# Ln and Exp over two chunks at once in a graph layer with routed experts: the adjacency stage on ScalarE, with its mask lead and one copy on VectorE moved

## What is computed

```
msg     = layernorm(x) @ W + B                       # x 8192x128
sens    = exp(-(1/adj - 1)**2 / (2 * 0.5**2))        # adj 8192x8192, most entries 0
weights = where(adj < 1, sens, 0)
x       = x + weights @ msg
z       = layernorm(x)
x       = x + layernorm(z + moe(z)) * gamma + beta   # 16 experts, top 2, 128 -> 256 -> 128, relu
```

## Time and profile before

| | us |
|---|---|
| median of 3 runs (1758.34 to 1759.6) | 1759.18 |
| the profiled execution's own time | 1758.88 |
| its span | 1757.1 |
| PE busy, of the span | 1624.8 (92%) |
| ACT busy | 1581.2 (90%) |
| DVE busy | 1525.8 (87%) |
| POOL busy | 430.1 (24%) |
| share of the 16 DMA engines taken by the loads' queue | 61.9% |
| a load of one chunk (1024 KB), from issue to landing, median | 5.3 |

### The profile page before, as it was taken

How to read it: one execution, slowest core, us unless ns; L and a number is a source line. 1 busy time by engine, 2 the same in 40 slices (tenths; PEclk the granted TensorE clock), 3 DMA queues, 4 the chain that set the end, 5 groups by cost and what they waited for, 6 DMA issues and landing times.

```text
span 1757.1 us, 23405 instructions
## 1 busy us (share of the span) xinstructions
PE 1624.8 (92%) x8178; PEld 1080.6 (61%) x8178; DVE 1525.8 (87%) x2278; ACT 1581.2 (90%) x1577; POOL 430.1 (24%) x309
## 2 busy tenths in 40 slices
PE   4889999999999999999999999999999999999840
PEld 3556666566656566656556656566656557999840
DVE  7999999999999999999999999999999994557876
ACT  5889999999999999999989999999999995666752
POOL 0000030303131313131304030303031301117775
PEclk9999999999999999999999999999999999999985
DMA  9447876667666666666867666667666842457653
GB/s 319 146 136 252 251 213 205 187 203 217 200 203 199 195 204 204 202 200 201 230 192 207 203 207 204 189 202 216 203 188 203 230 123 77 149 156 227 193 152 97
DMA packets 208500, 341.91 MB, mean 195 GB/s; under 512 B 18224, under 2 KB 65840, under 8 KB 208256
## 3 DMA queue, kind: packets, MB, share of 16 engines
q1 hardware_dynamic: 200064, 323.30, 61.9%
q0 software_dynamic: 8320, 17.12, 3.2%
HBM read 304.38 MB, written 35.98 MB: 194 GB/s over the span
## 4 chain that ended last, share of the span: by engine, by line
PE 44%; ACT 28%; DVE 12%; issue 11%; POOL 4%; DMA 1%; POOLq 0%; SPq 0%; DVEq 0%; ACTq 0%
PE acc L1033 22%; PE tp L1052 11%; ACT chunk L467 10%; ACT chunk L462 9%; ACT wT L473 8%; PE tp L1082 4%; PE tp L1095 4%; POOL chunk L446 4%; DVE chunk L595 4%; DVE chunk L589 4%; PE tp L1071 1%; PE misc L985 1%; DVE stats L601 1%; DVE msg L650 1%; DMA xs<-in_x_dram 1%
## 5 line engine op out<-in xcount | busy, mean ns | idle before, releaser
L1033 PE MATMUL acc<-wT,msg 128*128 128x512 f32 x2048 | 973.0, 598 | 16.2 <-DVE yT L681 16.2
L595 DVE SCALAR_TENSOR_TENSOR chunk<-chunk 128x2048 f32<-128x2048 f32 x256 | 585.6, 2287 | 98.2 <-ACT chunk L467 98.0
L1052 PEld LDWEIGHTS tp<-ident,chunk 128*128 128x128 f32 x4096 | 484.1, 142 | 226.2 <-issue 214.7
L473 ACT ACTIVATE wT<-tp 128x1024 f32<-128x1024 f32 x512 | 570.4, 1114 | 22.4 <-PE tp L1052 22.4
L589 DVE SCALAR_TENSOR_TENSOR chunk<-chunk 128x2048 f32<-128x2048 f32 x256 | 584.0, 2282 | 1.9 <-DMA chunk<-in_adj_dram 1.9
L1052 PE MATMUL tp<-ident,chunk 128*128 128x128 f32 x4096 | 538.5, 275 | 0.0
L462 ACT ACTIVATE chunk<-chunk 128x2048 f32<-128x2048 f32 x256 | 514.9, 2011 | 11.9 <-DVE chunk L589 11.9
L1033 PEld LDWEIGHTS acc<-wT,msg 128*128 128x128 f32 x2048 | 351.6, 192 | 267.7 <-issue 267.0
L467 ACT ACTIVATE chunk<-chunk 128x2048 f32<-128x2048 f32 x256 | 513.7, 2007 | 0.0
L418 POOL TENSOR_TENSOR pool_carrier<-pool_carrier 1x1 f32<-1x1 f32 x32 | 8.6, 270 | 1232.0 <-DVE row_now L766 1189.5
L428 POOL DMA_INDIRECT rows_in<-y,row_now x128 | 286.6, 2239 | 44.7 <-issue 44.7
(11 more groups left out here) (106 smaller groups left out, 574.8 us busy)
## 6 DMA issues: line engine op xcount, KB each, us to landing
chunk<-in_adj_dram SPq DMA_DIRECT2D x256, 1024.0 KB, 5.3
chunk<-rows_in SPq DMA_DIRECT2D x88, 128.0 KB, 2.1
rows_out<-chunk SPq DMA_DIRECT2D x88, 128.0 KB
y_kept<-y SPq DMA_DIRECT2D x16, 256.0 KB, 6.1
rows_in<-zeros SPq DMA_DIRECT2D x32, 128.0 KB
chunk<-y_kept SPq DMA_DIRECT2D x16, 256.0 KB, 3.4
out_dram<-chunk SPq DMA_DIRECT2D x16, 256.0 KB, 2.6
blobs<-in_L_ffn_w_dram SPq DMA_DIRECT2D x1, 2048.0 KB, 12.0
```

Of the source, the lines that this page charges most:

```text
L473: act.activation(wT[:, (g * PPG + m) % WSLOTS, :], tp[(g * PPG + m) % TSLOTS][:, :], ACT.Exp, scale=-2.0).then_inc(weighted, 1)
L595: dve.scalar_tensor_tensor(out=slot(c), in0=slot(c), scalar=2.0, in1=slot(c), op0=ALU.subtract, op1=ALU.mult).then_inc(squared, 1)
L1033: ins = pe.matmul(acc[:, :], msg[:, n, :], wT[:, (g * PPG + m) % WSLOTS, k * ROWS:(k + 1) * ROWS], start=(n == 0), stop=(n == 2 * PPG - 1))
L1052: ins = pe.transpose(tp[s % TSLOTS][:, t * ROWS + b * P:t * ROWS + (b + 1) * P], chunk[:, c % RING, b, j:j + P], ident[:, :])
```

## The change

From chunk 1 of group 1 on, Ln and Exp run over two neighbouring chunks in one instruction of 4096 elements a partition. Ln of a pair stands in the even step of an odd chunk (chunks c + 3 and c + 4), Exp of a pair in the even step of an even chunk (chunks c + 2 and c + 3); the odd steps have neither. Masks lead by five chunks from group 1 on, with one extra mask at its start. DVE's copy of the finished sum stands before the square of step 1, where it stood before the mask of step 2.

```
-    SQUARE_LEAD, LOG_LEAD, MASK_LEAD = 2, 3, 4
+    SQUARE_LEAD, LOG_LEAD, MASK_LEAD, PAIR_LEAD = 2, 3, 4, 5

+            def two(c):
+                return chunk[:, c % RING:c % RING + 2, :, :].rearrange("p r b j -> p (r b j)")
+
+            def log_two(g, c):
+                act.wait_ge(masked, g * CHUNKS + c + 2)
+                act.activation(two(c), two(c), ACT.Ln, bias=TINY).then_inc(logged, 2)
+
+            def invert_two(g, c):
+                act.wait_ge(logged, g * CHUNKS + c + 2)
+                act.activation(two(c), two(c), ACT.Exp, scale=-1.0).then_inc(inverted, 2)

@@ ScalarE, step m of group g, behind weigh(g, m)
-                    n = c + LOG_LEAD
-                    if not (g == GROUPS - 1 and n >= CHUNKS):
+                    if g == 0 or (g == 1 and c == 0):
+                        n = c + LOG_LEAD
                         (log if k == 0 else invert)(g + n // CHUNKS, n % CHUNKS)
+                    elif k == 0:
+                        n = c + (LOG_LEAD if c % 2 else LOG_LEAD - 1)
+                        if not (g == GROUPS - 1 and n >= CHUNKS):
+                            (log_two if c % 2 else invert_two)(g + n // CHUNKS, n % CHUNKS)

@@ VectorE, step m of group g
-                    if g and m == BEHIND:
+                    if g and m == BEHIND - 1:
                         gate_sum(g - 1)
                     c, k = divmod(m, PAIRS)
-                    n = c + (MASK_LEAD if k == 0 else SQUARE_LEAD)
+                    if g == 1 and m == 0:
+                        mask(g, MASK_LEAD)
+                    n = c + (SQUARE_LEAD if k else MASK_LEAD if g == 0 else PAIR_LEAD)
```

## The result

| | before | with the change |
|---|---|---|
| median, us | 1759.39 | 1797.51 (1793.64 to 1800.13, 4 runs) |
| span of the profiled execution | 1757.1 | 1791.9 |
| last copy of a sum (`gate_sum`) starts at | 1470.6 | 1505.6 |
| ACT busy | 1581.2 | 1564.5 |
| DVE busy | 1525.8 | 1521.0 |

The ratio is 1.0218, with a 95% interval of 1.02 to 1.0236: slower, by 38 us (forecast: 44, range 1773 to 1826). The adjacency stage ends 35.0 us later and what follows takes as long as before, 286.3 us against 286.5.

A forecast was written before the change was run, and what follows sets the result against it. ACT was taken as the bound, busy for all 87.3 us of a group. Merge -1.44, waits +3.17 and clock +1.1 gave +2.8 us a group, +43.9 in all: 1803 us, range 1773 to 1826.

The forecast's parts named there:

- Part 1: Merged Ln and Exp on ACT: a pair takes 3.51 us instead of 3.60, 16 pairs fewer a group, -1.44 us.
- Part 2: Squares start later on DVE: ACT stands 1.60 and 0.53 us after late `y`, 1.04 for `hot_ready`, +3.17 a group.
- Part 3: TensorE's clock falls at the wait for `y` in two of three groups, 1.63 us each: +1.1 us a group.
- PEclk below 1.00 in more than half of the groups: Sign in the changed profile: TensorE's clock row is below full in over half of the groups.
- Part 4: DVE's copy in step 1 fits in before the square; PE waits some 0.5 us at most, counted as 0.
- the rival of the late copy: DVE reaches step 1 late in every group, PE waits 2 us more: 28 us more, 1831 us; chance 0.07.
- Part 5: Masks at lead 5, one extra in group 1, and their loads: same mask cost, no load late, counted as 0.
- The sum: Whole kernel: +2.8 us a group over 14 groups, 4.3 in the last, +43.9 in all, 1803 us.
- DVE's lateness is absorbed: DVE's chains to `y` and `hot_ready` keep ahead, so only -1.44 us a group counts: 1739 us; chance 0.12.

The follow-up runs named there:

- the last version: The change with routing from the turn of `y` to the one-hot sums one step later, ranking and what follows two steps later: 1736.55 us, ratio 0.9877.
- only Ln: The change with only Ln over pairs, Exp over one chunk in its old place: 1864.51 us, ratio 0.9957 to the kernel before.
- only Exp: The change with only Exp over pairs, the two Lns apart in an odd chunk's steps: 1929.26 us, ratio 1.0308 to the kernel before.
- only the ranking moved: The change with only the ranking and what follows it one step later: 1779.06 us, ratio 1.0118 to the kernel before.
- the late copy: The change with DVE's copy of the sum put back to step 2: 1851.99 us, ratio 1.0533; in an earlier set 1969.46 against 1873.44 us.
- unmerged kernel: The change with Ln and Exp of one chunk each in their old places, masks and copy as changed: 1872.58 against 1873.44 us, ratio 0.9991.
- the kernel before with later routing: The kernel before, nothing merged, routing from the turn of `y` one step later, from the ranking on two: 1865.78 against 1873.02 us, ratio 0.9963.
- the kernel with the routing one step later: The change with the routing from the turn of `y` on one step later on PE, DVE and ACT: 1755.31 against 1758.12 us, ratio 0.9983.

## Why the prediction was right

- **Part 1**, the merge: forecast a slot of 3.51 us and -1.44 us a group; measured 3.51 us, and -1.53 us where nothing is in the way (the last version, with both moves). The rule that I set against it, of the Trainium skill's page "VectorE: DVE Perf Modes", section on the trn2 errata (0.187 us an instruction, 3.0 us a group), does not hold here: the slots of 2048 and 4096 elements, 1.80 and 3.51 us, leave 0.09.
- **Part 2**, the three gaps of ACT: forecast 1.60, 0.53 and 1.04, in all 3.17 us; by starts 1.42, 0.57 and 1.10, in all 3.09. The links fit one by one: square 3.81 us after the pair's Exp (forecast 3.76), 11.89 us from there to `y` (11.90). Together with Part 1: +1.77 us a group by the windows, +1.73 forecast. This agreement is a little better than that of the terms: the merge saved 0.1 more, the gaps cost 0.1 less, and the guess took 0.16 more, which the working did not have. The kernels with only Ln, only Exp, only the ranking moved and both moved show that this chain is the cause, and that it can be lifted.
- **Part 3**, the clock: **the term that was mis-sized.** Forecast a fall in two of three groups, 1.1 us a group. A fall after the wait for `y` costs 1.70 us (90.83 against 89.13), near the 1.63 taken, but it came in three of the 13 ordinary groups (in four of 13 in a second trace of the same kernel): 0.4 to 0.5 us a group. The sign "PEclk below 1.00 in more than half of the groups" did not come. The reading behind the term was wrong too: PE waited 1.96 us for the copy in six of the 13 ordinary groups before, not in all, and the clock fell in five of these six; in the other seven it waited 0 to 1.40 us, and the clock did not fall. Read rightly, the row would have given a larger share than two in three. So the price of a fall carried over from the rows, and how often it falls did not.
- **Part 4**, the copy: no wait of PE for it is left; DVE waits 0.2 to 0.8 us for PE there. Without the move PE stands 3.35 us, as said; it would have cost 56 us, twice the 28 us that the rival of the late copy was given.
- **Part 5**, masks and loads: nothing, as forecast. The unmerged kernel shows it directly.
- **The sum**, by copies of the sum: groups 1 to 8, +18.4 us (forecast 22.6); group 9, +3.2 (2.8); groups 10 to 14, +10.9 (14.2); the last group, +3.2 (4.3). In all +35.7, 8.2 us below the forecast, and this is the difference of two errors. The clock was forecast with 16.5 us. The trace has five falls, but two of them stand in groups 9 and 15, where the kernel before has one each as well; three are new, 5.1 us: 11.4 too high. The other terms were 3.2 too low: groups 1 and 10 took only 85.87 and 86.73 us before, so they lost more than the others, and group 9 lost 3.2 us without a further fall of the clock (the unmerged kernel loses 1.1 there, too). That group 9 came near its 2.8 is luck: 1.1 of the 2.8 was for the clock.

Of the rivals, "DVE's lateness is absorbed" (1739 us) did not decide here, because the routing stood where the squares are late. The kernel with both moves takes 1736.55 us, but that it lies so near is partly chance: 19.1 us of its gain are the merge's in the ordinary groups, and in the two table groups the moves take 9.4 us off and the merge puts 7.0 on.

## What to carry to other kernels

When lists in order on several engines are tied by semaphores, an instruction that is made longer delays what it releases, not only what stands behind it: before merging two, follow the chain from its result to the next wait of the bounding engine, by durations of the trace, and compare it with that engine's own way there. Idle time of 7 us a group on DVE did not help against a chain without a gap that was 1.5 us too long. If the chain is late, try to move the asker by a step: here that turned +38 us into -22, with the saving in full in the ordinary groups. Moving asker and producer together gained nothing for the ranking. And measure the same move without the merge, since a part of what it brings may be its own: 7.2 of these 21.9 us were.

## What I had not expected of the hardware

- How often TensorE's clock falls after such waits does not follow from their length alone. Of ordinary groups, by PE's idle time: 1.96 us ahead of the first products, five of six before and four of six in the kernel before with later routing; 2.40 us ahead of turning `y`, three of 12 in each of the two traces of the change; 2.52 us there, five of 11 (the ranking alone moved); about 3.35 us ahead of the first products, eight of 12, during the wait or right behind it (the late copy). After waits of less than 1.9 us no fall stood in an ordinary group of these traces. What else decides was not tried. A fall that cost nothing before was not free for PE either: in the group behind it, PE's wait for the copy was 0.33 to 0.36 us instead of 1.96, and 1.96 less the 1.63 of a fall is 0.33. So it was paid from PE's lead on ACT. Group 4 of the kernel before, right behind a group with a fall; the wait of 1.96 us is in the earlier trace rows:

```profile
415.83 1.96 PE L1033 MATMUL acc<-wT,msg 128*128 128x512 f32 x4 [0.33 <-DVE yT L681]
```

  Here is PE in a half-clock stretch of the changed kernel, with 3.58 us for products that take 1.88 at full clock:

```profile
355.36 0.66 PE L991 MATMUL misc<-ident,y 128*128 128x128 f32 x4 [2.40 <-DVE y L719]
...
355.86 1.06 PE L1071 MATMUL tp<-ident,chunk 128*128 128x128 f32 x8
...
356.73 3.58 PE L1052 MATMUL acc<-wT,msg 128*128 128x512 f32 x4
```

  The runs of the change spread by 6.5 us (1793.64 to 1800.13), those of the version without these waits by 0.8 us (1736.12 to 1736.96). Of the four runs of the change, the shortest has the highest mean granted clock (0.979) and the longest the lowest (0.973), so falls of the clock would fit as the cause. Against it, the kernel with the routing one step later spreads by 4.2 us without a fall in an ordinary group of its trace. It was not settled.
- The experts' part, which moves rows by DMA, took 286 us in two of the sets and in the comparison itself, and 400 to 409 us in the two others, with the adjacency stage unchanged. The cause of that was not tried.
